# The last stage of a transformer layer, unrolled: projection two chunks ahead, transposes in front of the down projection, low parts on POOL

## What is computed

```python
q, k, v = split(x @ w_qkv + b_qkv)            # rotary embedding on q and k
out = softmax(q @ k.T / sqrt(16)) @ v
x = layernorm(x + out @ w_out + b_out)
gate, up = x @ wg.T, x @ wu.T                 # weights: int32 in [-127, 127], times 1/127
x = layernorm(x + (silu(gate) * up) @ wd.T)
```

## Time and profile before

| | us |
|---|---|
| median of 3 runs | 3018.66 (3018.37 to 3021.16) |
| the profiled execution, its own time | 3021.53 |
| its span, first to last instruction | 3019.7 |
| PE busy in the span | 2895.0 (96%) |
| DVE busy | 2858.9 (95%) |
| ACT busy | 2541.5 (84%) |
| POOL busy | 292.0 (10%) |
| mean granted clock of TensorE | 0.977 |

### The profile page before, as it was taken

One profiled execution on the slowest core, in us unless ns is written; L12 is line 12 of the kernel. 1 busy time (PEld: TensorE's weight loads), 2 busy tenths in 40 slices (PEclk: granted clock), 3 DMA queues, 4 the chain that ended last, 5 costly groups with the idle time before them and its releaser, 6 DMA issues. The chain is left out here.

```text
span 3019.7 us, 66824 instructions
## 1 busy us (share of the span) xinstructions
PE 2895.0 (96%) x27022; PEld 901.6 (30%) x27022; DVE 2858.9 (95%) x3220; ACT 2541.5 (84%) x4587; POOL 292.0 (10%) x346
## 2 busy tenths in 40 slices
PE   7879999999999999999999999999999999889988
PEld 4541222222222222222222222222222222255555
DVE  8989999999999999999999999999999999478887
ACT  2444999999999999999999999999999999845554
POOL 2330000000000000000000000000000000144442
PEclk9986999999999999999999999999999999999999
DMA  4340111111111111111111111111111111233321
GB/s 146 128 155 17 33 34 36 36 35 36 35 35 35 34 35 34 34 33 34 34 34 34 34 34 33 34 37 34 36 36 34 35 35 30 59 84 96 93 85 35
DMA packets 120833, 145.55 MB, mean 48 GB/s; under 512 B 52576, under 2 KB 86752, under 8 KB 120544
## 3 DMA queue, kind: packets, MB, share of 16 engines
q1 hardware_dynamic: 120256, 141.51, 15.8%
q10 hardware_dynamic: 288, 0.01, 0.0%
HBM read 105.78 MB, written 35.13 MB: 47 GB/s over the span
## 5 line engine op out<-in xcount | busy, mean ns | idle before, releaser
L856 ACT ACTIVATE probs<-st_ps 128x512 f32<-128x512 f32 x4096 | 2228.0, 596 | 144.0 <-PE st_ps L772 74.5
L879 DVE TENSOR_REDUCE tile_max<-s_ps 128x1 f32<-128x1024 f32 x2048 | 2329.0, 1214 | 1.8 <-PE s_ps L758 1.7
L783 PE MATMUL o_ps<-probs,kept_v 128*17 128x256 f32 x16384 | 1282.8, 385 | 22.6 <-ACT sums L843 22.6
L758 PE MATMUL s_ps<-k,q 64*128 64x512 f16 x4096 | 1251.5, 386 | 22.4 <-PEq L93 12.2
L772 PE MATMUL st_ps<-q,k 64*128 64x512 f16 x4096 | 1246.5, 382 | 0.0
L783 PEld LDWEIGHTS o_ps<-probs,kept_v 128*17 128x17 f32 x16384 | 273.8, 95 | 887.7 <-issue 453.8
L772 PEld LDWEIGHTS st_ps<-q,k 64*128 64x128 f16 x4096 | 273.1, 93 | 868.5 <-ACT probs L856 866.7
L758 PEld LDWEIGHTS s_ps<-k,q 64*128 64x128 f16 x4096 | 233.2, 94 | 81.9 <-DVE tile_max L879 62.9
L956 POOL TENSOR_SCALAR max_scaled<-neg_max_t 128x32 f32<-128x32 f32 x64 | 18.4, 288 | 2304.6 <-DVE neg_max_t L890 2304.6
L1078 PE MATMUL p_ps<-w_down_half,h_high 128*128 128x256 f16 x384 | 104.4, 309 | 27.7 <-DVE h_low L1211 26.8
L227 PE MATMUL qk_ps<-x_t,w_qkv 128*128 128x512 f32 x256 | 117.4, 610 | 13.5 <-DVE turned_ps L340 7.2
(11 more groups left out here) (99 smaller groups left out, 1353.6 us busy)
## 6 DMA issues: line engine op xcount, KB each, us to landing
q<-q_parts SPq DMA_DIRECT2D x192, 128.0 KB
k<-k_parts SPq DMA_DIRECT2D x192, 128.0 KB
x_t<-in_x_t SPq DMA_DIRECT2D x16, 512.0 KB, 7.5
q_parts<-parts SPq DMA_DIRECT2D x32, 256.0 KB, 2.6
k_parts<-parts SPq DMA_DIRECT2D x32, 256.0 KB, 2.6
heads_out<-sums SPq DMA_DIRECT2D x256, 32.0 KB, 2.0
kept_v<-heads_out SPq DMA_DIRECT2D x16, 512.0 KB, 4.6
kept_v<-inverses_out SPq DMA_DIRECT2D x32, 256.0 KB
```

What stands on the lines that cost most here:

```text
L758: mm = pe.matmul(s_ps[g % 2][:, j * BANK:(j + 1) * BANK], q[h % 2][FIRST, r // KW * P:(r // KW + 1) * P], k[h % 2][FIRST, at:at + BANK], s ...
L783: mm = pe.matmul(o_ps[c * 32:c * 32 + VM, at:at + HALF], t["kept"][:, h, kt, :], probs[(h * KT + kt) % RING][:, c * BANK + at:c * BANK + a ...
L856: act.activation(probs[(h * KT + kt) % RING][:, c * BANK:(c + 1) * BANK], st_ps[n % ST][:, :], ACT.Exp, scale=scale).then_inc(exp_done, 1)
L879: dve.tensor_reduce(tile_max[h % 2][:, r // KW, r % KW:r % KW + 1], s_ps[g % 2][:, :], AX.X, ALU.max).then_inc(s_read, 1)
```

## The change

- The hardware loop goes: all 16 chunks are written out on every engine, with plain numbers in the waits.
- The output projection runs two chunks ahead (`AHEAD`), between feature tiles 1 and 2 of gate and up. Those of chunks 0 and 1 are done in `attend`, which also sums and averages z of chunk 1 behind the normalising of chunk 0.
- The transposes of chunk c+1 stand between up and down of chunk c, and the first ones in front of the branch on the register; ACT takes them over behind the last high part, in front of the table loads.
- The down product goes by feature tiles: tile m for all four token tiles, each with its wait for `h_low`.
- The last low part of the hidden activations is POOL's as well, and DVE's list is in a new order.
- Loads, `divide` and `bias` run three chunks ahead.

```diff
         @block.tensor
...
+                def down(c):
+
+                    wait(pe, y_done, 2 * c)
+                    if c + AHEAD < NCH:
+                        pe.wait_ge(z_done, 2 * (c + AHEAD + 1))
+                    for m in range(HT):
+                        pe.wait_ge(h_low_done, c * HT + m + 1)
                         for n in range(TT):
...
+                            mm = product(p_ps[:, n, :], pairs, m == 0 and n % 2 == 0, m == HT - 1 and n % 2 == 1)
+                            if m == HT - 1 and n % 2 == 1:
+                                mm.then_inc(down_done, 1)
+
+                for c in range(NCH):
                     pe.wait_ge(x1_low_done, KD * (c + 1))
                     for m in range(HT):
...
+                        gate_and_up(c, m)
+                        if m == 1 and c + AHEAD < NCH:
+                            steps["output_projection"](pe, c + AHEAD, p_ps)
+                    if c + 1 < NCH:
+                        transpose(c + 1)
+                    down(c)
+
+            transpose(0)
             wide = pe.value_load(f["wide_int"][0:1, 0:1], min_val=0, max_val=P)
```

ACT, `finish`:

```diff
+            load_silu()
+            take_transposed(0)
+            for c in range(NCH):
                 for m in range(HT):
...
                     if m > 0:
                         high(c, m - 1)
                 high(c, HT - 1)
-                steps["deviations"](act, c + 1)
-                if not last:
+                if c + 1 < NCH:
+                    take_transposed(c + 1)
+                steps["deviations"](act, c + AHEAD)
+                if c + 1 < NCH:
                     load_silu()
```

DVE, `finish`:

```diff
+            low(0)
+            for c in range(NCH):
+                if c > 0:
+                    sum_y(c - 1)
                 hide(c, 0)
...
+                steps["invert"](dve, c + 1, c + 1, c - 2)
+                if c + 1 < NCH:
+                    steps["normalize"](dve, x1[(c + 1) % 2], f["z"], 0, x1_done)
+                hide(c, 1)
+                if c > 1:
+                    second_norm(c - 2)
+                if c + AHEAD < NCH:
+                    steps["sum_z"](dve, c + AHEAD, p_ps)
+                hide(c, 2)
+                if c + AHEAD < NCH:
+                    steps["count_z"](dve, c + AHEAD)
+                if c == 0:
                     out["invert"](dve, HEADS - 1)
...
+                hide(c, 3)
+                if c > 0:
+                    moments_y(c - 1)
+                if c + AHEAD < NCH:
+                    steps["average_z"](dve, c + AHEAD)
+                steps["variances"](dve, c + AHEAD, min(c + AHEAD + 1, NCH), c)
+                hide(c, 4)
+                hide(c, 5)
+                if c + 1 < NCH:
+                    low(c + 1)
```

POOL and SP, `finish`:

```diff
+            steps["divide"](pool, AHEAD)
+            steps["bias"](pool, AHEAD)
+            for c in range(NCH):
+                if c + AHEAD + 1 < NCH:
+                    steps["divide"](pool, c + AHEAD + 1)
+                    steps["bias"](pool, c + AHEAD + 1)
+                for m in range(HT):
                     pool.wait_ge(h_high_done, c * HT + m + 1)
...
+            steps["load"](sp, AHEAD)
+            out["keep"](sp, HEADS - 1)
+            for c in range(NCH):
+                if c + AHEAD + 1 < NCH:
+                    steps["load"](sp, c + AHEAD + 1)
+                if c == 0:
                     out["inverses"](sp, HEADS - 1)
...
+                if c > 1:
+                    keep(c - 2)
```

`attend`, PE and DVE:

```diff
-                    if h == HEADS - 1 and n % 2 == 1 and n // 2 >= KT - TT:
-                        if n // 2 == KT - TT:
-                            pe.wait_ge(s_read, TILES)
-                        steps["output_projection"](pe, 0, 0, p_first, [n // 2 - KT + TT])
+                    if h == HEADS - 1 and n >= EXPS // 2 - 2 * TT:
+                        c, tile = divmod(n - EXPS // 2 + 2 * TT, TT)
+                        if tile == 0:
+                            pe.wait_ge(s_read, TILES - 1 + c)
+                        steps["output_projection"](pe, c, p_first[c], [tile])
...
+            for c in range(2):
+                steps["sum_z"](dve, c, p_first[c])
+                steps["count_z"](dve, c)
+                steps["average_z"](dve, c)
+                steps["variances"](dve, c, c + 1, 0)
+                if c == 0:
+                    steps["invert"](dve, 0, 0, 0)
+                    steps["normalize"](dve, f["x1"][0], f["z"], 0, f["x1_done"])
```

More of the change, by code:

```diff
@@ L568, in normalize @@
         last.then_inc(done, 1)
[L570 to L573, removed]
+    return dict(load=load, divide=divide, bias=bias, sum_z=sum_z, count=count,
+                output_projection=output_projection, average=average, count_z=count_z,
+                average_z=average_z, variances=variances, deviations=deviations, invert=invert,
+                normalize=normalize)
 def unit_state(ctx, nc, T):
@@ L668, in attend @@
         TT = WIDE // D
-        p_first = s_ps[0][:, :].rearrange("p (n d) -> p n d", n=TT)
+        p_first = [s_ps[c][:, :].rearrange("p (n d) -> p n d", n=TT) for c in range(2)]
         all_ones = sem("all_ones")
@@ L972, in _ @@
             for c in range(2):
-                steps["divide"](pool, c, c)
-                steps["bias"](pool, c, c)
+                steps["divide"](pool, c)
+                steps["bias"](pool, c)
 def finish(nc, t, w, f, u, B, T, D, HID):
@@ L1048, in _, with keep @@
         def _(sp):
[L1049 to L1052, removed]
+            def keep(c):
+                sp.wait_ge(result_done, c + 1)
+                sp.dma_start(t["out"].rearrange("(n p) d -> p n d", p=P)[:, c * TT:(c + 1) * TT, :],
+                             result[c % 2][:, :, :]).then_inc(kept[c % 2], 16)
+            steps["load"](sp, AHEAD)
[4 more added lines that the diff above has]
+                if c == 0:
                     out["inverses"](sp, HEADS - 1)
@@ L1055, in body, with transpose @@
                     sp.wait_ge(u["inverses_out"][1], HEADS // 2 * 16)
[L1056 to L1069, removed]
+                if c > 1:
+                    keep(c - 2)
+            keep(NCH - 2)
+            keep(NCH - 1)
+            for i in range(2):
+                sp.wait_ge(kept[i], NCH // 2 * 16)
         @block.tensor
         def _(pe):
+            def transpose(c):
+                pe.wait_ge(x1_done, c + 1)
+                wait(pe, x1_t_done, KD * c)
+                for kd in range(KD):
+                    for n in range(TT):
+                        mm = pe.transpose(t_ps[:, kd, n * P:(n + 1) * P], x1[c % 2][:, n, kd * P:(kd + 1) * P],
+                                          w["ident"][:, :])
+                    mm.then_inc(turned, 1)
             def ffn(wide):
@@ L1114, in body @@
[L1114 to L1130, removed]
@@ L1260, in _ @@
+            sum_y(NCH - 1)
+            steps["invert"](dve, NCH + 1, NCH, NCH - 2)
+            second_norm(NCH - 2)
+            moments_y(NCH - 1)
+            steps["variances"](dve, NCH + AHEAD, NCH, NCH)
+            steps["invert"](dve, NCH + AHEAD, NCH, NCH - 1)
+            second_norm(NCH - 1)
         @block.gpsimd
         def _(pool):
-            def body(c, par, first, last):
-                if not isinstance(c, int) or c + 2 < NCH:
-                    steps["divide"](pool, c + 2, par)
-                    steps["bias"](pool, c + 2, par)
-                for m in range(HT - 1):
+            steps["divide"](pool, AHEAD)
```

176 lines of the change are left out of this document (56 added, 120 removed).

## The result

The changed kernel takes 2986.95 us (2985.02 to 2987.79, 4 runs) against 3019.91 before (3018.37 to 3021.36, 4 runs): ratio 0.9887, 95% interval 0.9875 to 0.9899. The forecast was 2988.4. The profiled execution has a span of 2983.2 and took 2985.02; the span before was 3019.7.

What follows compares the result with a forecast made beforehand. The last stage was held by DVE waiting while POOL works from SBUF (the lock), plus a halved PE clock. Start, early chunks, ten of 21.5, last chunks and tail sum to 2989.4, 30.3 under 3019.7; 3018.66 - 30.3 = 2988.4 us, range 2980 to 2997.

Steps and rivals of the forecast that it cites:

- The old wait: Last stage: PE's 2.4 us wait per chunk for the last h_low goes, covered by 40 down matmuls and the transposes.
- the 3.98 that a chunk lost: Last-stage chunk of 23.90 against 19.92 of PE work: PE stands 2.4 us, then a halved clock costs 1.58.
- The new wait: Steady chunks: PE stands 1.57 us before the first gate, since DVE's second low part of x waits for POOL's divide.
- Rivals A: Steady chunks: the lock is free when low 1 comes, so chunks take 19.92, total 2973; chance 0.16.
- C: Steady chunks: POOL goes from divide straight to bias, PE stands 3.9 and the clock falls, total 3028; chance 0.06.
- Rival E: Whole kernel: little comes of it, start and early chunks worse by 10 beside B, 3014 and up; chance 0.06.
- Its size: Steady chunks: PE's wait for the second low part of x put at 1.57 us, making a chunk 21.5.
- The start: Entry from attention: last block starts some 8 us later, at 2640.4 not 2632.4, with the first gate at 2645.2.
- PE's wait for load 2 in chunk 0: Chunk 0: load 2's divide ends at 2651.9, so PE waits about 1 us for it and ends the projection at 2655.4.
- Rival B: Steady chunks: the clock falls at each new wait, 1.58 more in each of 10 chunks, total 3004; chance 0.18.
- Rival D: Hardware loop: branches do cost, 4.4 us for each of six turns, so unrolling saves 26 more, 2962; chance 0.04.

Runs made afterwards that it cites:

- run 2: Kernel before the change, with only the last low part of the hidden activations moved to POOL, in the old order: 3024.37 us, ratio 1.001.
- run 3: Changed kernel with the last low part of the hidden activations back on DVE: 3012.04 us, ratio 0.9977.
- run 4: Changed kernel with the transposes of the next chunk behind the down projection instead of in front: 3054.68 us, ratio 1.0109.
- run 5: Changed kernel with DVE computing the low parts of x from the transposes' PSUM tile instead of two SBUF tiles: 2977.34 us, ratio 0.9862.
- run 6: Changed kernel with POOL's divide and bias behind the chunk's first low part instead of in front of it: 3012.75 us, ratio 0.9976.
- run 10: Changed kernel with the transposes of chunk 0 behind the branch on the register again: 2992.72 us, ratio 0.9904.
- run 1: Kernel before the change, with only its last stage written out, 16 chunks without hardware loop: 3019.57 us, ratio 0.9997.

## Why the prediction was right

*The old wait and the clock.* Both parts of the 3.98 that a chunk lost are gone, by the steps given: down has 40 matmuls and the transposes in front of the eight that wait, and the clock stays at 1.00. Run 2 shows that the last low part on POOL isn't enough by itself, run 3 that the change needs it, and run 4 that it needs the transposes in front of the down product. No run takes out the new order of the down product, or that of DVE's list, alone, so what these are worth isn't shown.

*The new wait* is where it was put, and by the turns that were put: low 0 behind the last low part of the hidden activations, then `divide`, then low 1 (1.06 and 2.67 long, forecast near 1 and 2.7). Run 5 takes away the hold and the wait with it; runs 2, 3, 6 and 10 move it to other DVE operations, each of which then stretches. Rivals A and C fall by the trace: low 1 doesn't slip in, and `bias` doesn't go ahead of it. Rival E falls with them, since chunk 2 begins as early as forecast.

*Its size* was the term that was off. PE stands 0.94 a chunk, not 1.57, and the steady chunk is 20.86, not 21.5: (2900.72 - 2692.12)/10. Of the 0.64, 0.37 is between `hide` 3 and `hide` 4: 2.87 measured, 1.31 + 1.93 = 3.24 in the sum. The sum took its terms from rows where each average stood alone. In the new order both stand in a row: the step from the count of y to the averages is 1.43, not 1.57, the averages take 0.68 up to the variance, not 0.76, and `hide` 4 follows the variance after 0.11, not 0.26. With up and `hide` 2 0.06 earlier DVE ends `hide` 5 at 15.16 of the chunk, not 15.58. POOL's last two low parts take 2.27 together, not 2.32. The last 0.15 is a turn counted too high: DVE's turn and `divide` behind it were put at 0.55 + 2.36 = 2.91, and take 2.76 (2793.05 to 2795.81). The prediction's own row of `bias` with a turn in it, 2.79, had shown that. Over ten chunks the 0.64 makes 6.4 us. The sum of the span is 2989.4 and the trace has 2983.2; chunk 2 began another 0.5 earlier than forecast, and what follows the start of chunk 12 is 0.7 longer.

*The nearness of the total is in part luck.* The gain is by the mechanism forecast, but the span was 6.2 off and the median only 1.5. The forecast took 30.3 off a median that was 2.9 under the profiled execution before; the profiled execution of the changed kernel is 1.9 under its median. These two, which come from the spread of the runs, cover 4.8 of the 6.2.

*The start* was 8.5 later (ACT's first instruction in the block is at 2640.94 and was at 2632.40; the forecast was 2640.4). The first gate came at 2646.90, not 2645.2: all of the 3.98 for register read and branch lies behind the end of the transposes, and none beside them. Chunk 2 even so began at 2692.12, forecast 2692.6, because errors cancel. PE's wait for load 2 in chunk 0, put at 1 us, isn't there, since PE itself was later. And chunk 1 is 20.98 long (from 2671.14), not 22.5: its `normalize` does stretch beside POOL, to 4.37, but PE doesn't wait for it.

*Rival B*, the clock: waits that the profile gives as 0.76 (it counts from the modelled end of the matmul before, 0.18 later than its slot) did no harm in any chunk. How near the forecast 1.57 would have come can be read only from other kernels: four waits recorded as 1.83 and 1.84 (run 6) were followed by the full clock, the one of 2.03 (run 10) by half of it.

*Rival D* is settled by run 1: without the loop's branches the time is the same. The Trainium skill (Runtime: NRT & Kernel Launch, Instruction fetch mechanics) says that a taken branch out of the prefetched code stalls for a fetch; run 1 shows nothing of it at the loop's branches. At the one branch into the block PE stands 3.98 us, and no run divides this between the register read and a fetch.

## What to carry to other kernels

When DVE and POOL both work out of SBUF, list for each long POOL instruction the DVE operations that can meet it: those with two SBUF operands, and `tensor_scalar` from SBUF to SBUF, stood until it ended in these traces, and got one turn between two POOL instructions. If one of them is on the path, see first whether it can take an operand from PSUM (run 5 gained 10 us) before moving work between the engines (runs 2, 3 and 6 lost 4.5 to 26 us beside the kernel that they started from). And move the parts of a pipeline together: output projection ahead without the transposes is slower than moving neither (run 4).

## What the runs showed that was not expected

The same wait of PE doesn't always cost the same: in run 2 waits of 2.2 to 2.3 in front of the transposes were followed by a halved clock in some chunks (transposes in 1.8 to 2.0) and by a full one in others (1.09). In run 3 waits of 2.40 were followed by a halved clock in seven chunks of ten, in run 6 waits of 2.6 in three of seven. In the kernel before the wait of 2.23 in front of the down product halved the clock all 12 times, yet this longer one, in front of the last chunk's first gate, didn't:

```profile
2993.95 0.39 PE L1078 MATMUL g_ps<-x_high,w_gate_half 128*128 128x512 f16 x1 [2.77 <-DVE x_low L1217]
```

The length of the wait alone doesn't tell. What else decides isn't shown.

`second_norm` stretches beside a single low part of POOL's by only 0.18: it took 1.56 in the changed kernel's chunk shown, and `normalize`, the same four operations with POOL idle, 1.38.
